# Third attention on Trainium2: scores of two heads as three fp32r products of key and query halves, keys rewritten in place, keys and values alternating

## Chip, core and metric

The kernel runs on one core of a Trainium2 chip. The metric is device time in microseconds (us) of one launch. The engines are PE (TensorE, matrix products; PEld is its weight load), ACT (ScalarE), DVE (VectorE), POOL (GpSimd) and SP (SyncE, which here issues DMA). Each runs its own instructions in order and waits for the others on semaphores.

## What is computed

Four layers, each an attention over a context of 375 rows and then a feed-forward part with experts, on x of 16 batches of 112 rows of 256. The change touches the attention of the third layer (called layer 2 in the code): 16 heads of 64, no mask.

```python
def _L2_xattn_ref(x, context, Wq, Wk, Wv, Wo, bo):
    H, DH = (16, 64)
    SCALE = DH ** (-0.5)
    b, nq, _ = x.shape
    nk = context.shape[1]
    q = (x @ Wq.T).reshape(b, nq, H, DH)
    k = (context @ Wk.T).reshape(b, nk, H, DH)
    v = (context @ Wv.T).reshape(b, nk, H, DH)
    sim = jnp.einsum('bihd,bjhd->bhij', q, k) * SCALE
    attn = jax.nn.softmax(sim, axis=-1)
    out = jnp.einsum('bhij,bjhd->bihd', attn, v).reshape(b, nq, H * DH)
    return out @ Wo.T + bo

x = x + _L2_xattn_ref(_layernorm(x, axis=-1), ctx_1024, L2_xattn_Wq, L2_xattn_Wk, L2_xattn_Wv, L2_xattn_Wo, L2_xattn_bo)
```

## The kernel before

`Att` holds what one attention layer does and in which order: its `plan` is a list of steps that every engine walks through, taking from it only what is its own. `att_tensor` turns the plan into PE's instructions, `att_vector` into DVE's, `att_scalar` into ACT's. So the place of an entry in the plan is its place on all engines at once, and an engine that waits for one entry holds up all that follow in its own list.

For the third attention (`t.halves`, since its width is 1024) the plan takes the 16 heads of a batch in eight steps of two heads, called steps 0 to 7 here. A step is, on PE:

- `scores` (L1056): for each of the two heads one fp32 matmul of 64 rows, 112 weights (queries) and 375 columns (keys). Even heads use rows 0 to 63, odd heads rows 64 to 127; the results go to banks 0 and 1. An fp32 matmul is four passes over its columns and has two records in the trace.
- `pv` (L1099): values times transposed probabilities of the two heads of two steps before.
- `turn` (L1068): transposes of the probabilities of the two heads of the step before, three pieces each.
- the `extras` of that step: projections ("gens") for the next batch and the end of the last one. Their results go to two banks in turn, 6 and 7, so that a projection waits until the one two before it has been carried off (`freed`).

The projections are: `k` (L975), one of eight key tiles, 128 x 376 in six fp32r passes (halved weights times halved context: upper times upper, upper times lower, lower times upper; fp32r is one pass over its columns); `v` (L979), one of six value tiles, 126 x 512, six such passes; `q` (L964), four of eight query tiles in fp32; `x` (L1014), transposes of two batches' normed input rows; `i` (L1001), transposes of the heads' reciprocal sums; `o` (L1005), the product with Wo; `n` (L1020), transposes of two batches' normed rows for the feed-forward part; `r` (L1027), its router. `i` is in step 1, `o` in step 3, `q` in step 0; `x` and `n` come once for two batches, `x` in step 6, `n` in step 7, `r` in the step 0 after it.

`steps` places them: `spread` deals them out over the slots of a batch by their costs, in the order queries, keys, output product, values (`post`), each not before its earliest slot.

Around the scores: DVE takes the minimum of a head's negated scores (L1285), ACT the exponential from the bank (L1327, with the row sum), PE transposes it in the next step, DVE copies that out (L1294), and `pv` uses it the step after. The scores of a head wait until the exponentials of the head two before have left its bank. After a batch's last head DVE takes the reciprocals of the sums (L1250) and spreads them over 1024 columns (L1258), which `i` transposes.

A key tile is carried off by ACT (L1373, a copy), queries by DVE (L1183, times the scale), both into buffers of two batches (`kTv`, `qmv`); values by ACT (L1379). DVE also splits the context of each batch into halves (`halve_context`, L721 and L723, in step 0), adds up the former layer's results (L763), and normalises rows (L785 for this attention, L1240 for the feed-forward part, `xn`).

Before the steps of batch 0 come its own projections: eight `k`, then six `v`, `x` and `q`. The weights of the values are halved by DVE at that point (`("wh", 1)`, `halve_values_weights`); PE's first value tile waits for it.

## Time and profile before

| | |
|---|---|
| runs | 2403.71 us median of 3 (2401.43 to 2405.17) |
| the profiled execution | 2400.26 us, of which the span of the trace is 2398.4 |
| PE busy | 2236.1 us (93%) |
| DVE busy | 1186.2 us (49%) |
| ACT busy | 1044.0 us (44%) |
| chain that ended last | PE 83%, DVE 7% |
| mean granted clock of PE | 0.97 |
| third attention | the steps with scores run from 1028 to 1722 us |

The busy shares are over the whole span. The chain that ended last is followed back from the last instruction, at each point to what released it. In a timeline each row is a start time, a duration, an engine, a line with operation and operands, and a count of instructions merged; in brackets stands how long the engine was idle before it and for what. The start of a PE row is the start of its first weight load, and PE's rows overlap a little, since a matmul's end is modelled: times between places on PE are best taken from start to start. In a table by windows, each row gives for one stretch its length, the busy time of each engine (with its count), the granted clock of PE, and DMA.

### The profile page before, as it was taken

Reading aid. Unit: us, or ns where it says so; the run is one execution under the profiler, and the core shown is the slowest. Engines: PE = TensorE matmul, PEld = TensorE weight load, DVE = VectorE, ACT = ScalarE, POOL = GpSimd, SP = SyncE. Lnnn points to the kernel's source line nnn. Section 1 sums busy time; section 2 is a strip of 40 time slices with the busy share of each in tenths; the row PEclk is TensorE's granted clock in tenths of the full one; section 3 lists DMA queues with packets and bytes.
Section 4 is the critical chain, followed back from the end, with each engine's and each line's share of the span. In section 5 each row is a group of like instructions: output and inputs, shape, how many; then the busy total and the mean of one; then the engine's idle time right before and its main releaser. Section 6 shows DMA issues by size and latency. Waiting matters only on the chain.

```text
span 2398.4 us, 44743 instructions
## 1 busy us (share of the span) xinstructions
PE 2236.1 (93%) x15310; PEld 1711.2 (71%) x15310; DVE 1186.2 (49%) x3453; ACT 1044.0 (44%) x2859; POOL 350.8 (15%) x393
## 2 busy tenths in 40 slices
PE   5999998999988899999999999999869979999998
PEld 4777877677766667777777777777647757777765
DVE  4777774222245522454554554554542256777613
ACT  3777773222223222244444444444312257778711
POOL 2000001111144255100000000000024310000020
PEclk8999998999999899999999999999979989999999
DMA  7666666222255322200000000010232177766400
GB/s 187 188 173 160 172 152 250 77 83 87 84 149 183 121 71 65 63 21 8 19 26 15 11 18 8 11 53 1 92 127 66 61 209 183 182 161 167 102 12 23
DMA packets 152698, 230.52 MB, mean 96 GB/s; under 512 B 66368, under 2 KB 127120, under 8 KB 149920
## 3 DMA queue, kind: packets, MB, share of 16 engines
q1 hardware_dynamic: 139808, 195.30, 28.5%
q0 software_dynamic: 10656, 29.37, 3.7%
q10 hardware_dynamic: 2016, 3.00, 0.5%
q8 instruction: 130, 2.13, 0.4%
q14 instruction: 88, 0.72, 0.1%
HBM read 176.36 MB, written 51.25 MB: 95 GB/s over the span
## 4 chain that ended last, share of the span: by engine, by line
PE 83%; DVE 7%; issue 3%; DMA 3%; ACT 1%; SPq 1%; POOL 1%; ACTq 0%; DVEq 0%; POOLq 0%
PE bank L1068 10%; PE bank L1859 9%; PE bank L1099 7%; PE bank L1892 6%; PE bank L979 6%; PE bank L975 6%; PE bank L1924 5%; PE bank L1005 4%; PE bank L1056 4%; PE bank L990 3%; PE bank L1051 3%; PE bank L964 3%; PE bank L1909 3%; PE bank L986 3%; PE bank L2208 2%
## 5 line engine op out<-in xcount | busy, mean ns | idle before, releaser
L1068 PE MATMUL bank<-ident,arena 112*125 112x112 f32 x2352 | 374.1, 277 | 4.6 <-ACT arena L1334 0.5
L1068 PEld LDWEIGHTS bank<-ident,arena 112*125 112x125 f32 x2352 | 336.2, 188 | 53.1 <-issue 13.1
L1327 ACT ACTIVATE arena<-arena,mx 112x375 f32<-112x375 f32 x512 | 309.5, 605 | 117.0 <-DVE mx L1273 114.6
L1273 DVE CUSTOM_DVE_ANT_0 arena<-bank,maskf 112x375 f32<-112x375 f32 x512 | 271.3, 541 | 125.9 <-PE bank L1051 124.6
L1051 PE MATMUL bank<-kS,qS 128*112 128x376 f32 x512 | 233.2, 456 | 33.6 <-DMA qS<-query_halves 24.1
L1327 ACT ACTIVATE arena<-bank,mx 112x375 f32<-112x375 f32 x272 | 156.1, 576 | 186.5 <-DVE mx L1285 155.4
L1285 DVE TENSOR_REDUCE mx<-bank 112x1 f32<-112x375 f32 x256 | 128.9, 543 | 211.8 <-PE bank L1056 211.7
L1859 PE MATMUL bank<-arena 128*128 x532 | 229.5, 554 | 2.7 <-ACT arena L1985 1.4
L1294 DVE COPY arena<-bank 125x336 f32<-125x336 f32 x448 | 214.2, 502 | 33.5 <-PE bank L1068 33.5
L1099 PEld LDWEIGHTS bank<-arena 125*32 125x32 f32 (+1 forms) x4608 | 144.5, 119 | 85.9 <-issue 68.5
L1099 PE MATMUL bank<-arena 125*32 125x112 f32 (+1 forms) x4608 | 202.6, 265 | 3.0 <-DVE arena L1294 2.9
L1334 ACT ACTIVATE arena<-bank 125x336 f32<-125x336 f32 x336 | 147.0, 438 | 47.0 <-PE bank L1068 43.4
L1892 PE MATMUL bank<-arena 128*128 (+1 forms) x672 | 167.1, 380 | 0.0
L979 PE MATMUL bank<-weight_halves,ctx_halves 128*126 128x512 f32 x576 | 150.3, 404 | 2.1 <-ACT arena L1379 2.1
L1485 POOL TENSOR_TENSOR rstd<-newton,root 112x2 f32<-112x2 f32 x32 | 22.5, 702 | 859.3 <-DVE newton L1229 859.2
L1859 PEld LDWEIGHTS bank<-arena 128*128 128x128 f32 x532 | 99.8, 191 | 65.0 <-issue 46.0
L975 PE MATMUL bank<-ctx_halves,weight_halves 128*128 128x376 f32 x768 | 143.6, 339 | 1.9 <-DVEq L715 1.9
L1924 PE MATMUL bank<-xnT,arena 128*128 128x224 f32 (+1 forms) x640 | 143.3, 369 | 0.3 <-DVEq L715 0.3
L1781 POOL DMA_INDIRECT results<-arena,scatter_id x91 | 89.9, 988 | 362.9 <-ACT arena L2007 285.0
L1051 PEld LDWEIGHTS bank<-kS,qS 128*112 128x112 f32 x512 | 91.3, 179 | 56.8 <-DMA qS<-query_halves 24.8
L975 PEld LDWEIGHTS bank<-ctx_halves,weight_halves 128*128 128x128 f32 x768 | 130.2, 188 | 2.3 <-DVEq L715 2.3
L1924 PEld LDWEIGHTS bank<-xnT,arena 128*128 128x128 f32 (+1 forms) x640 | 112.4, 181 | 24.9 <-issue 11.6
(243 smaller groups left out, 3416.4 us busy)
## 6 DMA issues: line engine op xcount, KB each, us to landing
kS<-key_halves SPq DMA_DIRECT2D x256, 188.0 KB, 3.8
key_halves<-arena SPq DMA_DIRECT2D x64, 376.0 KB, 4.1
arena<-in_ctxT SPq DMA_DIRECT2D x63, 376.0 KB, 4.5
arena<-in_f_out SPq DMA_DIRECT2D x21, 768.0 KB, 4.6
qS<-query_halves SPq DMA_DIRECT2D x256, 56.0 KB, 2.2
arena<-in_f_up SPq DMA_DIRECT2D x4, 2816.0 KB
arena<-results SPq DMA_DIRECT2D x38, 224.0 KB, 4.4
query_halves<-arena SPq DMA_DIRECT2D x32, 224.0 KB, 2.8
```

The source lines that it names most:

```text
L975: m = pe.matmul(dst[:, 0:SKE], wH[:, 0, wh, c * t.W + o * P:c * t.W + (o + 1) * P], ctxH[:, ch, c, :], **flags)
L979: m = pe.matmul(dst[0:KT + 1, 0:t.VW], ctxH[:, ch, c, o * KT:(o + 1) * KT + 1], wH[:, 1, wh, c * t.W + h * t.VW:c * t.W + (h + 1) * t.VW], ...
L1051: m = pe.matmul(bank[g % 2][0:S, 0:SKE], qS[:, b % 2, h * S:(h + 1) * S].bitcast(F32R), kS[:, b % 2, h // 2 * SKE:(h // 2 + 1) * SKE].bitc ...
L1068: m = pe.transpose(bank[2 + g % 2][0:KT, k * S:(k + 1) * S], pr[:, g % t.NR, k * KT:(k + 1) * KT], ident[0:S, 0:S])
L1099: m = pe.matmul(out, v, pTv(t, g + j)[:, k, :], **flags)
L1273: dve.tensor_tensor_reduce(sm[:, g % 2, :], bank[g % 2][0:S, 0:SK], maskf[:, :], -t.a["scale"], 3e38, ALU.add, ALU.min, mx[:, g % t.NR:g % ...
L1294: dve.tensor_copy(pTb(t, g), bank[2 + g % 2][0:KT, 0:NKT * S]).then_inc(t.pt_sbuf[1], 1)
L1327: act.activation(pr[:, g % t.NR, :], src, ACT.Exp, bias=mx[:, g % t.NR:g % t.NR + 1], scale=-1.0, accum_out=row_sum(t, b)[:, h:h + 1]).the ...
L1334: act.activation(pTb(t, g), bank[2 + g % 2][0:KT, 0:NKT * S], ACT.Copy).then_inc(t.pt_sbuf[0], 1)
L1859: ins = pe.matmul(bank[m % 2][:, 0:w * f.NU], xTb(n)[:, k, :], up[:, bass.ds(expert[n], 1), at:at + w * f.NU].rearrange("p e n -> p (e n)" ...
L1892: ins = pe.matmul(bank[4 + n % 2][:, 0:D], midT_of(f, m)[:, j * P:(j + 1) * P], w2, start=(q + j == 0), stop=(q == G - 1 and j == J - 1))
L1924: ins = pe.matmul(bank[f.hidden_bank[s]][0:w, u * 2 * S:(u + 1) * 2 * S], up[u][:, k, o:o + w], xnT[:, k, c * 2 * S:(c + 1) * 2 * S], star ...
```

## The change

Queries and keys of the third attention are held as two fp32r halves each, an upper half rounded to fp32r and the rest as lower half. The scores of a head become three fp32r matmuls that add up in its bank: upper query times upper key, upper times lower, lower times upper. They are issued for the two heads of a step in turn (bank 0 and 1), each of 64 rows, 112 weights and 376 columns. The first of the pair waits for both exponentials of the step before.

The halves: ACT writes the upper half of a key tile or of four query tiles from the bank (for queries with the scale), and DVE then writes bank minus upper half as the lower half and frees the bank. Keys have one buffer for all batches: tile o of the next batch is written over tile o of this one, and so its projection may stand only behind the scores of the pair that uses it (step o). `turns_of_keys` lays out the projections of a batch accordingly: queries, then keys and values in turn, with the output product between; each key not before slot 2o. The halving of a batch's context waits for the last key and the last value tile.

```diff
+        def turns_of_keys(w, q, k, v, out):
+            k = [(step, cost, w + 2 * step[3]) for step, cost, _ in k]
+            if not k:
+                return out
+            return (q + k[0:1] + v[0:1] + k[1:2] + v[1:2] + k[2:3] + v[2:3] + k[3:4] + out + k[4:5] + v[3:4] + k[5:6]
+                    + v[4:5] + k[6:7] + v[5:6] + k[7:8])
...
-                    spread(items + done[:cut] + post, w, H - 1)
+                    spread(items + (turns_of_keys(w, q, k, post, done[:cut]) if self.halves else done[:cut] + post), w, H - 1)
...
+        kH = within(KT_AT, "key_halves_2", [P, 2, 8, SKE], F32R)
+        qH = within(QM_AT, "query_halves_2", [P, 2, 2, 8, S], F32R)
...
-            return t.g0 + t.gen_index("v", b, NKT - 1, t.VH - 1) + 1
+            return t.g0 + max(t.gen_index("k", b, t.NO - 1), t.gen_index("v", b, NKT - 1, t.VH - 1)) + 1
...
+                    if t.halves and h % 2:
+                        continue
...
-                    elif h == 0:
-                        freed_all(pe, t, "q", b)
-                        freed_all(pe, t, "k", b)
+                    elif t.halves:
+                        if h == 0:
+                            freed_all(pe, t, "q", b)
+                        freed(pe, t, t.gen_index("k", b, h // 2))
                     if g >= 2:
-                        pe.wait_ge(t.maxed if t.masked else t.probs, t.h0 + g - 1)
+                        pe.wait_ge(t.maxed if t.masked else t.probs, t.h0 + g - 1 + t.halves)
...
                     elif t.halves:
-                        rows = slice(h % 2 * dh, (h % 2 + 1) * dh)
-                        m = pe.matmul(bank[g % 2][0:S, 0:SK], qmv(t, b)[rows, h // 2, :], kTv(t, b)[rows, h // 2, :],
-                                      start=True, stop=True)
+                        for n, (qh, kh) in enumerate(((0, 0), (0, 1), (1, 0))):
+                            for j in range(2):
+                                rows = slice(j * dh, (j + 1) * dh)
+                                m = pe.matmul(bank[j][0:S, 0:SKE], qH[rows, b % 2, qh, h // 2, :], kH[rows, kh, h // 2, :],
+                                              start=(n == 0), stop=(n == 2))
+                                if n == 2:
+                                    m.then_inc(t.scores, 1)
+                        continue
...
+                if t.halves and kind in "qk":
+                    dve.wait_ge(t.upper, t.u0 + t.upper_of[(kind, b, o, h)])
+                    if kind == "q":
+                        ins = dve.scalar_tensor_tensor(out=qH[:, b % 2, 1, o:o + t.QG, :],
+                                                       in0=src[:, 0:t.QG * S].rearrange("p (o t) -> p o t", t=S),
+                                                       scalar=qscale, in1=qH[:, b % 2, 0, o:o + t.QG, :].bitcast(F32),
+                                                       op0=ALU.mult, op1=ALU.subtract)
+                    else:
+                        ins = dve.tensor_tensor(kH[:, 1, o, :], src[:, 0:SKE], kH[:, 0, o, :].bitcast(F32), ALU.subtract)
+                    ins.then_inc(t.gen_free[n % t.GB], 1)
+                    return
...
+                if kind in "qk" and t.halves:
+                    if kind == "q":
+                        ins = act.activation(qH[:, b % 2, 0, o:o + t.QG, :],
+                                             src[:, 0:t.QG * S].rearrange("p (o t) -> p o t", t=S), ACT.Copy,
+                                             scale=-t.a["scale"])
+                    else:
+                        ins = act.activation(kH[:, 0, o, :], src[:, 0:SKE], ACT.Copy)
+                    ins.then_inc(t.upper, 1)
+                    return
...
-                elif kind == "k":
-                    ins = act.activation(kTv(t, b)[:, o, :], src[:, 0:SK], ACT.Copy)
```

What this does to the order of instructions is shown at three places. Lines of the changed kernel are some 14 to 30 higher: scores are L1075, products with values L1121, transposes of probabilities L1090, keys L989, values L993, queries L978, normed rows' transposes L1034, reciprocals' transposes L1015.

PE, step 7 of batch 2 and the scores after it (`ident,xn` is the transpose of the normed rows). Before:

```order
L1056 MATMUL bank<-arena 112x375 x2
L1099 MATMUL bank<-arena 64x112 x6
L1068 MATMUL bank<-ident,arena 125x112 x6
L979 MATMUL bank<-weight_halves,ctx_halves 126x512 x6
L1020 MATMUL bank<-ident,xn 128x112 x4
L1056 MATMUL bank<-arena 112x375 x2
```

After:

```order
L1075 MATMUL bank<-key_halves,query_halves 112x376 x6
L1121 MATMUL bank<-arena 64x112 x6
L1090 MATMUL bank<-ident,arena 125x112 x6
L989 MATMUL bank<-ctx_halves,weight_halves 128x376 x6
L1034 MATMUL bank<-ident,xn 128x112 x4
L1075 MATMUL bank<-key_halves,query_halves 112x376 x6
```

The value tile ahead of the transpose has become the last key tile, and the two matmuls of a pair have become six.

DVE from the same step 7 to the reciprocals of step 1 (`xn` is the normed rows, `lgt` the router's logits, `rinv` the reciprocals; L1294 and L1323 copy transposed probabilities). Before:

```order
L1294 COPY arena<-bank 125x336 x2
L1240 TENSOR_SCALAR xn<-x,rstd,nmr 112x256 x2
L1285 TENSOR_REDUCE mx<-bank 112x1 x2
L1294 COPY arena<-bank 125x336 x2
L763 SCALAR_TENSOR_TENSOR x<-arena,t_0,x 112x256
L721 CAST ctx_halves<-arena 128x752
L723 TENSOR_TENSOR ctx_halves<-arena,ctx_halves 128x752
L1183 TENSOR_SCALAR arena<-bank 128x448
L763 SCALAR_TENSOR_TENSOR x<-arena,t_0,x 112x256
L1207 TENSOR_TENSOR lgt<-bank,brB 112x16
L1183 TENSOR_SCALAR arena<-bank 128x448
L1250 RECIPROCAL rinv<-sums 112x16
```

After:

```order
L1209 TENSOR_TENSOR key_halves<-bank,key_halves 128x376
L1269 TENSOR_SCALAR xn<-x,rstd,nmr 112x256 x2
L1314 TENSOR_REDUCE mx<-bank 112x1 x2
L1323 COPY arena<-bank 125x336 x2
L777 SCALAR_TENSOR_TENSOR x<-arena,t_0,x 112x256
L735 CAST ctx_halves<-arena 128x752
L737 TENSOR_TENSOR ctx_halves<-arena,ctx_halves 128x752
L1204 SCALAR_TENSOR_TENSOR query_halves<-bank,query_halves 128x448
L777 SCALAR_TENSOR_TENSOR x<-arena,t_0,x 112x256
L1236 TENSOR_TENSOR lgt<-bank,brB 112x16
L1204 SCALAR_TENSOR_TENSOR query_halves<-bank,query_halves 128x448
L1279 RECIPROCAL rinv<-sums 112x16
```

The lower half of a key tile (L1209) now stands ahead of the normed rows. Those of the queries (L1204) stand where their scaling stood, the second right ahead of the reciprocals.

DVE at the start of the stage, from the first normed rows to the first scores. Before:

```order
L785 TENSOR_SCALAR on<-x,rstd,nmr 112x256 x2
L721 CAST weight_halves<-arena 128x2048
L723 TENSOR_TENSOR weight_halves<-arena,weight_halves 128x2048
L1183 TENSOR_SCALAR arena<-bank 128x448 x2
L1285 TENSOR_REDUCE mx<-bank 112x1 x2
```

After:

```order
L799 TENSOR_SCALAR on<-x,rstd,nmr 112x256 x2
L1209 TENSOR_TENSOR key_halves<-bank,key_halves 128x376 x8
L735 CAST weight_halves<-arena 128x2048
L737 TENSOR_TENSOR weight_halves<-arena,weight_halves 128x2048
L1204 SCALAR_TENSOR_TENSOR query_halves<-bank,query_halves 128x448 x2
L1314 TENSOR_REDUCE mx<-bank 112x1 x2
```

Eight lower halves of keys now stand ahead of the halving of the values' weights.

## Rows read from the trace of the kernel before

**Rows 1.** Windows over the third attention: length, engines' busy us (count), clock, DMA.
```profile
1028.00:1722.00 694.00, 686.16 (x4978) 528.79 (x4977) 351.27 (x788) 298.60 (x762) 23.86 (x28) 1.00 0.07 23
```
**Rows 2.** PE timeline, batch 4, steps 0 and 1: start, us, engine, line, count, idle before.
```profile
1201.76 0.89 PE L1056 MATMUL bank<-arena 64*112 64x375 f32 x4
...
1204.05 3.74 PE L964 MATMUL bank<-xnT,arena 128*128 128x112 f32 x32
1207.72 0.89 PE L1056 MATMUL bank<-arena 64*112 64x375 f32 x4
1208.54 0.80 PE L1099 MATMUL bank<-arena 125*64 125x112 f32 x12
1209.48 0.96 PE L1001 MATMUL bank<-ident,on 112*128 112x112 f32 x8 [0.15 <-DVE on L1258]
```
**Rows 3.** PE timeline at the start of the stage.
```profile
1005.26 8.47 PE L975 MATMUL bank<-ctx_halves,weight_halves 128*128 128x376 f32 x48 [1.86 <-DVEq L715]
1013.58 8.53 PE L979 MATMUL bank<-weight_halves,ctx_halves 128*126 128x512 f32 x36
```
**Rows 4.** PE timeline of batch 15 and the end of the stage.
```profile
1675.04 3.61 PE L1005 MATMUL bank<-arena,oT 128*112 128x256 f32 x16
...
1718.58 1.44 PE L1056 MATMUL bank<-arena 64*112 64x375 f32 x4
1719.94 0.80 PE L1099 MATMUL bank<-arena 125*64 125x112 f32 x12
...
1731.07 5.30 PE L1005 MATMUL bank<-arena,oT 128*112 128x256 f32 x16 [1.53 <-DVE oT L1175]
```
**Rows 5.** ACT timeline, second exponential of the pair at 1201.76, its sum.
```profile
1204.46 0.19 ACT L1327 ACTIVATION_READ_ACCUMULATOR arena<-bank,mx 112x1 f32 x1
```
**Rows 6.** PEld timeline, the weight loads of one pair.
```profile
1219.61 0.27 PEld L1056 LDWEIGHTS bank<-arena 64*112 64x112 f32 x4 [0.24 <-issue]
```
**Rows 7.** Groups by line and form: count, busy us, mean ns, idle before.
```profile
L1373 ACT ACTIVATE arena<-bank 128x375 f32<-128x375 f32 x128 | 62.0, 484 | 69.5 <-PE bank L975 69.4
L1384 ACT ACTIVATE xnT<-bank 128x448 f32<-128x448 f32 x64 | 34.0, 536 | 47.4 <-PE bank L1020 35.1 <-PE bank L1014 12.2
L1164 DVE TENSOR_TENSOR arena<-bank,arena 128x375 fp32r<-128x375 f32 x32 | 17.2, 538 | 1.1 <-ACT arena L1358 1.1
...
L763 DVE SCALAR_TENSOR_TENSOR x<-arena,t,x 112x256 f32<-112x256 f32 x20 | 9.1, 475 | 0.0
```
**Rows 8.** DVE timeline in step 1, second queries and the reciprocals' copy.
```profile
1207.83 0.62 DVE L1183 TENSOR_SCALAR arena<-bank 128x448 f32<-128x448 f32 x1 [1.01 <-PE bank L964]
...
1208.64 0.69 DVE L1258 COPY on<-rinv 112x1024 f32<-112x1024 f32 x1
```
**Rows 9.** ACT timeline, the copy of a key tile.
```profile
1219.72 0.48 ACT L1373 ACTIVATE arena<-bank 128x375 f32<-128x375 f32 x1 [0.54 <-PE bank L975]
```
**Rows 10.** DVE timeline in a step 7 with normed rows.
```profile
1244.69 0.73 DVE L1240 TENSOR_SCALAR xn<-x,rstd,nmr 112x256 f32<-112x256 f32 x2
```
**Rows 11.** PE timeline, batches 4 and 5: normed rows, router, rows' transposes.
```profile
1245.56 0.57 PE L1020 MATMUL bank<-ident,xn 112*128 112x112 f32 x4
...
1251.56 2.04 PE L964 MATMUL bank<-xnT,arena 128*128 128x112 f32 x16 [0.56 <-DVE arena L1183]
...
1286.00 0.55 PE L1014 MATMUL bank<-ident,arena 112*128 112x112 f32 x4
1286.85 1.66 PE L979 MATMUL bank<-weight_halves,ctx_halves 128*126 128x512 f32 x6 [0.30 <-ACT arena L1379]
```
**Rows 12.** DVE timeline at the start of the stage, halving of the values' weights.
```profile
1005.30 1.23 DVE L721 CAST weight_halves<-arena 128x2048 fp32r<-128x2048 f32 x1
1006.56 3.27 DVE L723 TENSOR_TENSOR weight_halves<-arena,weight_halves 128x2048 fp32r<-128x2048 f32 x1
```
**Rows 13.** Windows, two short stretches: the clock is third from the end.
```profile
1732.00:1734.00 2.00, 2.00 (x6) 1.49 (x5) 0.00 (x0) 0.00 (x0) 0.00 (x0) 0.50 0.00 0
1004.00:1005.00 1.00, 0.00 (x0) 0.00 (x0) 0.93 (x4) 0.00 (x0) 0.12 (x1) 1.00 0.00 0
```

More of the change, by code:

```diff
@@ L144, in __init__ @@
         self.index = {s[1:5]: s[5] for s in self.gens}
+        self.upper_of = {s[1:5]: n + 1 for n, s in enumerate(s for s in self.gens if s[1] in "qk")}
         self.in_steps = {s[1:]: n + 1 for n, s in enumerate(
@@ L149, in __init__ @@
         if self.halves:
-            self.halved = sems["halved"]
+            self.halved, self.upper = sems["halved"], sems["upper"]
+            self.u0 = 3 * B
         if self.stack:
             self.spilled, self.upper = sems["spilled"], sems["upper"]
-            self.u0 = 3 * B if L else 0
+            self.u0 = 3 * B + 10 * B if L else 0
             self.s0 = 16 * B if L else 0
@@ L285, in steps @@
                     q, k, post = self.proj(b + 1)
-                    items += ([(("ctx", b + 1), 0, 0)] if self.halves else []) + q + k
+                    if self.halves:
+                        items = [(("ctx", b + 1), 0, 0)]
+                    else:
+                        items += q + k
                 else:
-                    post = []
+                    q, k, post = [], [], []
                 if b:
@@ L291, in steps @@
                     cut = done.index((("stats", b - 1), 0, w + pv_lag)) + 1
-                    spread(items + done[:cut] + post, w, H - 1)
+                    spread(items + (turns_of_keys(w, q, k, post, done[:cut]) if self.halves else done[:cut] + post), w, H - 1)
                     follow(b - 1, done[cut:])
                 else:
-                    spread(items + post, w, H - 1)
+                    spread(items + (turns_of_keys(w, q, k, post, []) if self.halves else post), w, H - 1)
             done = self.late(B - 1, G + pv_lag)
@@ L1178, in gen @@
                     return
-                if kind in "knx" or (kind == "v" and not t.a["bv"]) or (kind == "q" and (H == 1 or t.stack)):
+                if t.halves and kind in "qk":
[9 more added lines that the diff above has]
+                    return
+                if kind in "qknx" or (kind == "v" and not t.a["bv"]):
                     return
                 dve.wait_ge(t.gen_ready, t.g0 + n + 1)
-                if kind == "q":
-                    ins = dve.tensor_scalar(qmv(t, b)[:, o:o + t.QG, :],
-                                            src[:, 0:t.QG * S].rearrange("p (o t) -> p o t", t=S),
-                                            qscale, None, ALU.mult)
-                elif kind == "v" and t.stack:
+                if kind == "v" and t.stack:
                     if b == 0 and o == 0:
@@ L1361, in gen @@
             def gen(kind, b, o, h, n):
-                if kind in "or" or (kind == "q" and H > 1 and not t.stack) or (kind == "v" and t.a["bv"]):
+                if kind in "or" or (kind == "v" and t.a["bv"]):
                     return
@@ L1368, in gen @@
                     return
+                if kind in "qk" and t.halves:
[3 more added lines that the diff above has]
+                                             scale=-t.a["scale"])
+                    else:
+                        ins = act.activation(kH[:, 0, o, :], src[:, 0:SKE], ACT.Copy)
+                    ins.then_inc(t.upper, 1)
+                    return
                 if kind == "q":
```

## The prediction

> **What bounds the kernel now.** I read the page's busy shares and its chain first: both are PE's for the most part. The change touches one stage, the third attention, so next came the windows over it: of 694 us PE is busy 686, DVE 351, ACT 299, at a granted clock of 1.00 [rows 1]. PE is the bound there: whatever shortens or delays its queue moves the end, while DVE and ACT have room on average. Then the PE timeline of one batch, which is where a wait on them would hurt. The reader should see in it that a batch is eight steps, each a pair of scores (L1056), products with values (L1099), two heads' transposes (L1068) and one to three projections, back to back, and that hardly a row carries idle time in brackets.
>
> **Scores, the gain.** A pair takes 0.82 us from its start to that of L1099 (1207.72 to 1208.54) [rows 2]. Two heads of four fp32 passes of 375 columns at 2.4 GHz are 1.25 us one after the other and 0.625 us side by side, so the two row halves do run side by side, and 0.195 us is entry and exit (the first weights, and the last columns leaving). After, each half does three single passes. One pass of this type over 376 columns has a row of its own: 48 of L975 in 8.32 us (1005.26 to 1013.58), 0.173 each [rows 3]. Is the 0.195 paid by the pair or by each of its two rounds of two passes? Where the heads of a pair ran one behind the other, four such rounds, the pair took 1.36 us (1718.58 to 1719.94) [rows 4], 0.11 above its 1.25: by the pair. So 0.195 + 3 x 0.173 = 0.71, by pure streaming (3 x 0.157) 0.665; were it by the round, 0.81. I take 0.70, near the first two: a gain of 0.12 a pair (0.11 to 0.155). It counts in the 120 pairs of batches 0 to 14: **-14.4 us** (-13 to -19). In batch 15 there are no projections, and a step is set by the exponentials: the second one ends 2.9 us after the start of its scores (from 1201.76 to 1204.46 + 0.19) [rows 2, 5], while scores, products and transposes take 2.2. Those eight I put at zero.
>
> The weights are now loaded six times a pair instead of four. The row shows the four loads done in 0.27 us [rows 6], so six would be under 0.45, hidden under the passes. The Trainium skill (TensorE: Matmul & The Clock Gate, LDWEIGHTS) gives the time of a load as its columns over 1.2 GHz, for 112 columns 93 ns. By that page's figure, six loads in line and the last pass behind them would make the pair 0.8 us, an estimate, and the gain nearly nothing; the row speaks for loads side by side.
>
> **Halving on ACT, then on DVE.** Keys were copied by ACT, queries scaled by DVE. Now ACT writes the upper half, and DVE, waiting for it, the lower. ACT: a key tile as before 0.484, and 32 new query copies of 0.536. DVE: 128 new subtractions of 0.538 [rows 7], queries 0.62 as before [rows 8]. That is 69 us more on DVE and 17 on ACT within 694, far below PE: nothing by load. What counts is how long a projection's bank (two, 6 and 7) is held, and what stands behind the halving on DVE. ACT starts 0.11 after PE has left a projection (1219.72, where PE's next work starts at 1219.61) [rows 6, 9]. DVE to PE takes 0.15 (1208.64 + 0.69 = 1209.33, to 1209.48) [rows 2, 8], for a bank some 0.10. ACT to DVE is not shown; I take 0.05, between 0 and 0.15. A key bank is free after 0.11 + 0.48 + 0.05 + 0.54 + 0.10 = **1.28 us**, against 0.69. Five places of PE's queue stand behind such a hand-over.
>
> 1. Step 1, 14 batches. PE's transposes of the reciprocals (L1001) wait for DVE's copy of them (L1258), which stands behind the second queries on DVE. The wait was 0.15 [rows 2]. DVE now starts on those queries 0.70 instead of 0.11 after they are ready, and PE arrives 0.12 sooner: 0.59 + 0.12 = 0.71, x14 = **+9.9**.
> 2. Step 7, 7 times. PE's transposes of the normed rows (L1020) wait for DVE's L1240. That ran at 1244.69 [rows 10], under a value projection, and PE went straight on at 1245.56 [rows 11]. In the new order the lower half of the last key tile stands ahead of it on DVE, and on PE nothing stands between that tile and the transposes. PE waits 0.11 + 0.48 + 0.05 + 0.54 + 0.73 + 0.15, less 0.06 of overlap, = 2.0, x7 = **+14.0**.
> 3. Step 6, 7 times. A transpose of rows (L1014, 0.55 less overlap) lies between two projections that share a bank: PE waited 0.30 [rows 11], now 1.28 - 0.50 = 0.78. 0.48 x 7 = **+3.4**.
> 4. Step 1 again: the third projection reuses the first's bank. The value tile between them takes 1.40, more than 1.28, but in 6 batches a DVE step of 0.47 (L763) [rows 7] is ahead and leaves about 0.33: x6 = **+2.0**. In the 6 batches with the router in step 0 the second queries wait on DVE already (0.56) [rows 11], so the pair's 0.12 isn't gained there: **+0.7**.
> 5. The start of the stage. Eight key tiles in a row on two banks: 1.28 against the 1.03 of the tile between, three times 0.25 = 0.75. Then the values need halved weights. DVE made them under the keys (1005.30 to 1009.83, 4.53 us) [rows 12]; the new order has them behind all eight lower halves: 0.11 + 0.48 + 0.05 + 0.54 + 4.53 + 0.10 = 5.8 of idle PE. First queries to scores: 0.59 more. Idle PE costs clock as well: 1.86 us of it before 1005.26 left the clock at 1.00 [rows 3, 13], but after the short gaps before 1731 it stood at 0.50, and L1005 took 5.30 for 3.61 [rows 4, 13]. I take that 1.7 once. **+8.8**.
>
> In the other steps no bank and no exponential is late: the shortest step, with one key tile, is 0.70 + 0.73 + 0.68 + 1.03 = 3.1, against 2.8 for both exponentials. The new wait for both at once is thus covered, by 0.3; without a projection it would cost as much as in batch 15. Rewriting keys in place adds no wait: a tile's projection stands behind its scores on PE. DMA is as before; the results of the former stage are asked for some 8 us later and are used as much later.
>
> **Sum.** 9.9 + 14.0 + 3.4 + 2.0 + 0.7 + 8.8 = 38.8, less 14.4: **+24.4 us**. The profiled execution took 2400.3 (span 2398.4); it would be 2424.7. The median of the runs is 3.4 higher, 2403.7, so I say **2428**.
>
> **Rivals.**
> - *Loads in line.* If the six loads of a pair follow one another at the 0.115 that a piece of the query projection takes (32 in 3.67 us, of which 0.093 each is streaming) [rows 2], the pair is 6 x 0.115 + 0.157 + 0.1 = 0.95, and 0.80 if half of that hides: 2440 to 2458. The skill's page above is for it, the four loads in 0.27 us against it. 8%.
> - *Halves not side by side* for this type: 0.195 + 6 x 0.173 = 1.23, +0.41 x 120 = +49 in place of -14.4: 2492. For it: no row has this type on half the rows. Against it: fp32 does it. 5%.
> - *The clock falls at the 7 waits of 2.0 us*: 1.7 each, +12: 2440. Against it: the 1.86 us at a clock of 1.00. 8%.
> - *The other side: entry and exit vanish.* If the first load and the drain hide under the neighbours (projections of the same type ahead, L1099 behind), a pair is 0.47 and the gain 0.35 x 120 = 42; 38.8 - 42 = -3: 2400.5. It ends under the time of before from 0.50 a pair on. For it: between projections nothing of the kind is paid. Against it: the 0.195 of the pairs in the trace. 7%; in more than half of that a small wait is less too, and it is over 0.2% faster.
> - *Waits half as dear* (a shorter subtraction or hand-over, no clock lost): 2406 to 2418. 12%.
> - That the change isn't made: the order shows six passes of the new type for each pair, so no.
>
> The forecast's own case, 2418 to 2440, has 60%. **Range** 2408 to 2450: halves, the dearest loads and the vanished entry are left out (some 18%), the clock is in. About 0.2% (4.8 us) is what a measurement of this kernel can tell from no change. Faster by more 5%, within it 9%, slower 86%.
>
> **What would show it.** Right: pairs 0.67 to 0.75 us long up to the values' products; PE idle in the stage up from 8 to about 45 us, with waits of about 2 us for DVE's normed rows, 0.9 for the reciprocals, and one of 5 to 6 us before the first value tile, for DVE's halving. Wrong: a pair at 0.80 or above (loads) or 1.2 (halves) or under 0.6 (entry); idle PE under 20 us; or a clock below 1.00 inside the stage after its first 30 us.

## The result, and the profile after

The changed kernel takes **2426.3 us** (median of four runs, 2423.7 to 2430.7), before 2404.4 (2401.4 to 2405.8): a ratio of 1.0102, interval 1.0089 to 1.0114 (the ratios here are the measurement's own, up to 0.0014 off the quotient of the medians, which is 1.0091 in this case). Forecast: 2428. Its profiled execution has a span of 2421.9 us, 23.5 more than before.

The first view is the windows from the start of the first scores of the third attention to that of the last, before and after: length, then busy time of PE, PEld, DVE, ACT, POOL, then the granted clock.

```profile
1027.83:1721.51 693.68, 685.85 (x4977) 528.70 (x4977) 350.78 (x787) 298.11 (x761) 23.86 (x28) 1.00 0.07 23
```
After:
```profile
1038.08:1748.80 710.72, 672.77 (x5230) 550.72 (x5231) 410.36 (x908) 310.25 (x793) 23.81 (x28) 1.00 0.07 23
```
PE is busy 13.1 us less and idle 30.1 us more (7.8 before, 37.95 after). The change does what it says, and its waits cost about twice what it saves: at full clock PE would be busy 16.9 us less, and 3.8 of these went to a slower clock (e8 below). The 23.5 us lie as follows: +1.1 before the stage, +9.1 from the first key products to the first scores, +17.0 from there to the last scores, -3.8 behind them.

The PE timeline of batches 4 and 5, after, answers to [rows 2] and [rows 11] (start, us, line, names, count, idle before and its releaser):

```profile
1209.02 1.66 PE L993 MATMUL bank<-weight_halves,ctx_halves 128*126 128x512 f32 x6 [0.77 <-DVE key_halves L1209]
...
1219.76 0.77 PE L1075 MATMUL bank<-key_halves,query_halves 64*112 64x376 f32 x6
1220.46 0.80 PE L1121 MATMUL bank<-arena 125*64 125x112 f32 x12
1222.10 0.96 PE L1015 MATMUL bank<-ident,on 112*128 112x112 f32 x8 [0.85 <-DVE on L1287]
...
1259.33 0.57 PE L1034 MATMUL bank<-ident,xn 112*128 112x112 f32 x4 [1.89 <-DVE xn L1269]
...
1265.24 2.04 PE L978 MATMUL bank<-xnT,arena 128*128 128x112 f32 x16 [0.59 <-DVE query_halves L1204]
```
A pair of scores takes 0.70 us up to the products with values (1219.76 to 1220.46), for 0.82. In exchange there is a wait at four of the places that the forecast named. Behind the last of a pair of batches' key tiles DVE first halves the tile, then writes the normed rows; DVE timeline, after, answering to [rows 10]:

```profile
1257.99 0.55 DVE L1209 TENSOR_TENSOR key_halves<-bank,key_halves 128x376 fp32r<-128x376 f32 x1 [0.90 <-ACT key_halves L1404]
1258.46 0.72 DVE L1269 TENSOR_SCALAR xn<-x,rstd,nmr 112x256 f32<-112x256 f32 x2
```
The view of PE's waits over the stage (1035 to 1746; total, times, longest):

```profile
PE bank L1034 <- DVE xn L1269: 13.2, 7, 1.9
PE bank L1015 <- DVE on L1287: 11.9, 14, 0.9
PE bank L993 <- DVE key_halves L1209: 5.4, 7, 0.8
PE bank L978 <- DVE query_halves L1204: 3.6, 6, 0.6
```
The six weight loads of a pair, on the row of PE's load queue that answers to [rows 6], take 0.44 us and lie under the products:

```profile
1219.76 0.44 PEld L1075 LDWEIGHTS bank<-key_halves,query_halves 64*112 64x112 f32 x6
```
The start of the stage, PE timeline, for [rows 3]:

```profile
1006.37 2.31 PE L989 MATMUL bank<-ctx_halves,weight_halves 128*128 128x376 f32 x12 [1.87 <-DVEq L729]
1008.95 7.24 PE L989 MATMUL bank<-ctx_halves,weight_halves 128*128 128x376 f32 x36 [0.27 <-DVE key_halves L1209]
1020.90 10.88 PE L993 MATMUL bank<-weight_halves,ctx_halves 128*126 128x512 f32 x36 [4.71 <-DVE weight_halves L737]
```
and its DVE timeline, for [rows 12]:

```profile
1017.21 1.22 DVE L735 CAST weight_halves<-arena 128x2048 fp32r<-128x2048 f32 x1
1018.46 2.29 DVE L737 TENSOR_TENSOR weight_halves<-arena,weight_halves 128x2048 fp32r<-128x2048 f32 x1
```
The long wait before the first value tile is there, and the 36 products behind it take 10.88 us for 8.53: their first third runs at clock 0.50.

One thing is there that the forecast named as a sign of being wrong, a clock below 1.00 inside the stage. Behind the third of the seven waits for normed rows the same matmuls get longer (PE timeline, after):

```profile
1351.91 0.57 PE L1034 MATMUL bank<-ident,xn 112*128 112x112 f32 x4 [1.89 <-DVE xn L1269]
1352.41 0.77 PE L1075 MATMUL bank<-key_halves,query_halves 64*112 64x376 f32 x6
1353.11 0.98 PE L1121 MATMUL bank<-arena 125*64 125x112 f32 x12
1354.02 1.60 PE L1090 MATMUL bank<-ident,arena 112*125 112x112 f32 x6
```
L1090 takes 1.60 for 0.91, and the window over it shows the clock, third from the end, at half (1.2 GHz):

```profile
1354.00:1356.00 2.00, 2.00 (x11) 1.98 (x10) 1.06 (x3) 1.13 (x4) 0.00 (x0) 0.50 0.04 15
```
It happens twice in this kernel, behind the third and the seventh of those waits.

### The profile page after: what moved, and what is told of

Same layout as the page of the kernel before. It is cut to its first block, busy times and chain, and to the rows that moved or that the text cites. A ratio compares the mean times of both kernels' runs of the same rounds, so it can differ in the third digit from the quotient of the medians.

```text
span 2421.9 us, 45521 instructions
## 1 busy us (share of the span) xinstructions
PE 2222.9 (92%) x15566; PEld 1731.2 (71%) x15566; DVE 1249.7 (52%) x3581; ACT 1055.9 (44%) x2891; POOL 349.5 (14%) x393
## 4 chain that ended last, share of the span: by engine, by line
PE 82%; DVE 8%; issue 3%; DMA 3%; ACT 2%; SPq 1%; POOL 1%; ACTq 0%; DVEq 0%; POOLq 0%
PE bank L1090 10%; PE bank L1895 9%; PE bank L1121 7%; PE bank L1928 6%; PE bank L993 6%; PE bank L989 5%; PE bank L1960 5%; PE bank L1019 4%; PE bank L978 3%; PE bank L1004 3%; PE bank L1068 3%; PE bank L1075 3%; PE bank L1945 3%; PE bank L1000 3%; PE bank L2244 2%
## 5 line engine op out<-in xcount | busy, mean ns | idle before, releaser
L1090 PE MATMUL bank<-ident,arena 112*125 112x112 f32 x2352 | 374.4, 277 | 4.9 <-ACT arena L1363 0.5
L1090 PEld LDWEIGHTS bank<-ident,arena 112*125 112x125 f32 x2352 | 336.6, 189 | 53.1 <-issue 13.4
L1323 DVE COPY arena<-bank 125x336 f32<-125x336 f32 x448 | 214.4, 502 | 19.6 <-PE bank L1090 19.5
L1121 PE MATMUL bank<-arena 125*32 125x112 f32 (+1 forms) x4608 | 203.3, 266 | 3.0 <-DVE arena L1323 2.9
L1121 PEld LDWEIGHTS bank<-arena 125*32 125x32 f32 (+1 forms) x4608 | 144.8, 119 | 49.7 <-issue 32.8
L993 PE MATMUL bank<-weight_halves,ctx_halves 128*126 128x512 f32 x576 | 155.1, 406 | 10.2 <-DVE key_halves L1209 5.4
L989 PE MATMUL bank<-ctx_halves,weight_halves 128*128 128x376 f32 x768 | 158.1, 342 | 2.6 <-DVEq L729 1.9
L1209 DVE TENSOR_TENSOR key_halves<-bank,key_halves 128x376 fp32r<-128x376 f32 x128 | 70.3, 549 | 161.2 <-ACT key_halves L1404 160.9
L989 PEld LDWEIGHTS bank<-ctx_halves,weight_halves 128*128 128x128 f32 x768 | 129.6, 188 | 12.1 <-DVE key_halves L1209 5.9
```

The costliest lines, as they stand in the source:

```text
L989: m = pe.matmul(dst[:, 0:SKE], wH[:, 0, wh, c * t.W + o * P:c * t.W + (o + 1) * P], ctxH[:, ch, c, :], **flags)
L993: m = pe.matmul(dst[0:KT + 1, 0:t.VW], ctxH[:, ch, c, o * KT:(o + 1) * KT + 1], wH[:, 1, wh, c * t.W + h * t.VW:c * t.W + (h + 1) * t.VW], ...
L1090: m = pe.transpose(bank[2 + g % 2][0:KT, k * S:(k + 1) * S], pr[:, g % t.NR, k * KT:(k + 1) * KT], ident[0:S, 0:S])
L1121: m = pe.matmul(out, v, pTv(t, g + j)[:, k, :], **flags)
L1323: dve.tensor_copy(pTb(t, g), bank[2 + g % 2][0:KT, 0:NKT * S]).then_inc(t.pt_sbuf[1], 1)
```

## Experiments

All kernels are edits of the changed one, save b1. "Idle" and "busy" are PE's between the first scores and the last. "Falls" counts the waits for normed rows behind which a window shows a clock under 0.97, of those in the stage; "behind" is the time from the last scores to the end of the span. All columns from the fourth on are of one profiled execution each, which in e5 and e8 was the slowest of eight and of ten (2409.7 and 2406.9 us), in after the fastest of four. Ratios are to before, measured beside each (2404.4 and 2404.3 for e1 to e7, 2403.0 for e8, e9 and b1).

| kernel | median us | ratio (interval) | first to last scores | idle | busy | falls | behind |
|---|---|---|---|---|---|---|---|
| before | 2404.4 | | 693.7 | 7.8 | 685.9 | | 676.9 |
| after | 2426.3 | 1.0102 (1.0089-1.0114) | 710.7 | 37.9 | 672.8 | 2 of 7 | 673.1 |
| e1 | 2425.3 | 1.0101 (1.0063-1.0140) | 712.2 | 37.9 | 674.2 | 3 of 7 | 673.5 |
| e1b | 2427.6 | 1.0100 (1.0080-1.0119) | 712.3 | 38.0 | 674.3 | 3 of 7 | 680.5 |
| e2 | 2412.8 | 1.0035 (1.0024-1.0047) | 697.1 | 27.5 | 669.7 | 0 of 7 | 673.0 |
| e3 | 2429.2 | 1.0099 (1.0082-1.0116) | 709.4 | 25.2 | 684.1 | 6 of 7 | 681.1 |
| e4 | 2392.1 | 0.9956 (0.9939-0.9973) | 677.4 | 10.2 | 667.2 | 0 of 7 | 679.9 |
| e5 | 2401.5 | 0.9983 (0.9967-1.0000) | 684.2 | 42.4 | 641.8 | 7 of 7 | 681.3 |
| e6 | 2438.3 | 1.0155 (1.0118-1.0193) | 716.5 | 37.1 | 679.4 | 3 of 7 | 680.4 |
| e7 | 2451.6 | 1.0211 (1.0173-1.0248) | 735.0 | 53.1 | 681.9 | 5 of 7 | 673.2 |
| e8 | 2403.0 | 1.0002 (0.9993-1.0012) | 684.6 | 15.7 | 669.0 | 0 of 7 | 677.4 |
| e9 | 2395.5 | 0.9964 (0.9950-0.9978) | 677.2 | 10.2 | 667.0 | 0 of 7 | 677.7 |
| b1 | 2425.0 | 1.0094 (1.0078-1.0111) | 714.7 | 19.4 | 695.3 | 6 of 6 | 677.7 |

**e5: the price of a product.**

```diff
-                        for n, (qh, kh) in enumerate(((0, 0), (0, 1), (1, 0))):
+                        for n, (qh, kh) in enumerate(((0, 0),)):
...
```


> The changed kernel with one of the three products of a head's scores, upper by upper, so two passes for a pair instead of six. The two others are left out. My theory: entry and exit (0.195 us) are paid by the pair, so it takes 0.195 + 0.17 = 0.37 us up to the values' products, against 0.70; 0.33 x 108 pairs (those ahead of a wait for DVE give nothing) = 36 us less than the change, some 2391. Rival: the cost is by the round (0.70 / 3), so the pair takes 0.23 and the time falls by 50.

PE timeline of e5:

```profile
1208.44 0.42 PE L1075 MATMUL bank<-key_halves,query_halves 64*112 64x376 f32 x2
1208.79 0.80 PE L1121 MATMUL bank<-arena 125*64 125x112 f32 x12
```
A pair with one product takes 0.35 us, with three 0.70: 0.175 a round and 0.18 of entry and exit, paid once. That is the forecast's model of a pair. But of the 42 us that 120 pairs give, only 31 are seen in PE's busy time (672.8 to 641.8): in the profiled execution the clock fell behind all seven waits. The median is 24.8 us under after's, where 36 were expected. PE's idle time grew too, since it now comes 0.35 us earlier to the reciprocals (their wait is 1.19 for 0.85).

**e6: are the halves side by side?**

```diff
-                        for n, (qh, kh) in enumerate(((0, 0), (0, 1), (1, 0))):
-                            for j in range(2):
+                        for j in range(2):
+                            for n, (qh, kh) in enumerate(((0, 0), (0, 1), (1, 0))):
```


> The changed kernel with the six products of a pair in another order: three of the first head, then three of the second. Theory: PE starts matmuls in order, so the second head's first starts only beside the first head's third: 0.31 + 0.47 + 0.195 = 0.98 us a pair, +0.28 x 108 = 30 us more than the change, some 2456. Rival: in the kernel before the pair was also written head after head, and took 0.82, as short as side by side: then 0.70 here too and no difference.

PE timeline of e6:

```profile
1206.21 0.77 PE L1075 MATMUL bank<-key_halves,query_halves 64*112 64x376 f32 x6
1206.91 0.80 PE L1121 MATMUL bank<-arena 125*64 125x112 f32 x12
```
The pair stays at 0.70 us, while six products in line would be 6 x 0.17 = 1.0. So the two row halves work side by side even where all of one head's products stand ahead of the other's. PE's idle time is after's (37.1 for 37.9). So its 12 us are not in the pairs. The profiled execution, 14.7 us longer than after's, has 6.6 us more busy time with the same matmuls and three falls of the clock, and 7.3 more behind the last scores (below). Whether this order makes the clock fall more often isn't shown.

**e2: the normed rows ahead of the last key tile.** In step 7 the transposes of the normed rows go to the front of the step's extras, so that DVE writes them before it halves the key.

```diff
-                extras[at].append(step)
+                if self.halves and step[0] == "ln" and step[2] == LN_STEPS:
+                    extras[at].insert(0, step)
+                else:
+                    extras[at].append(step)
```


> The changed kernel with one DVE step moved: in the 7 steps with a transpose of normed rows, DVE normalises the rows before the lower half of the last key tile, not after. My theory: the 7 waits of 1.9 us (13.2 us) go and nothing takes their place, since DVE is idle there while PE makes the key tile: 13 us less than the change, some 2413; with the one fall of the clock that follows such a wait in batch 15 up to 15. Rival: the key's lower half, now later, delays the minimum of the next scores and by it PE: less than 6 us gained.

PE timeline of e2:

```profile
1257.66 0.57 PE L1037 MATMUL bank<-ident,xn 112*128 112x112 f32 x4 [0.45 <-DVE xn L1272]
```
The wait is 0.45 for 1.89 (0.38 to 0.45 in all seven), PE's idle time falls by 10.5 us (7 x 1.5), and no fall of the clock is left in the stage after its start: another 3.1 of busy time. 13.5 us in the median, as expected.

**e3: the reciprocals ahead of the second queries.**

```diff
-                if last:
+                if last and g >= G:
                     plan.append(("norm", (g - 2 * lag) // H))
...
-                plan += extras[g] + extras[g + 1]
+                both = extras[g] + extras[g + 1]
+                if g and g % H == 0 and g + 2 < G + 2 * lag and g < G:
+                    at = max([n for n, s in enumerate(both) if s[:2] == ("gen", "q")] or [0])
+                    both.insert(at, ("norm", g // H - 1))
+                plan += both
```


> The changed kernel with the reciprocals and their copy (DVE) moved from behind the second queries of step 0 to ahead of them, where DVE waits for PE. My theory: the 14 waits of 0.85 us for DVE's copy (11.9 us) go: 10 to 12 us less than the change, some 2415. Rival: the second queries, then later on DVE, hold their bank, and the transposes of the reciprocals wait for that instead: under 4 us gained.

A miss: 3 us slower, not 10 to 12 faster. Yet the step did what it should. Windows, first to last scores:

```profile
1037.22:1746.57 709.35, 684.13 (x5230) 560.56 (x5231) 410.98 (x908) 310.34 (x793) 23.85 (x28) 0.98 0.07 23
```
Idle time fell by 12.7 us, all fourteen waits are gone; the same matmuls are busy 11.4 us longer. The PE timeline shows where, behind a wait of the same 1.89 us:

```profile
1256.40 0.57 PE L1038 MATMUL bank<-ident,xn 112*128 112x112 f32 x4 [1.89 <-DVE xn L1273]
1256.91 1.10 PE L1079 MATMUL bank<-key_halves,query_halves 64*112 64x376 f32 x6
1257.94 1.39 PE L1125 MATMUL bank<-arena 125*64 125x112 f32 x12
```
L1125 takes 1.39 for 0.80, and the window behind it has the clock at half:

```profile
1258.00:1260.00 2.00, 2.00 (x17) 1.72 (x16) 1.00 (x2) 0.66 (x2) 0.00 (x0) 0.50 0.26 86
```
So it goes behind six of the seven waits. From one wait for normed rows to the next, two batches, e3 needs 90.84 us where no fall is between (1535.04 to 1625.88) and 92.38 with one (1256.40 to 1348.78); after needs 92.6 without. The step gained 1.8 us per two batches, and a fall gave back 1.5, in two of the six more: there the clock stayed low for some 7 and 14 us.

**e8: e2 and e3 together**, which takes away what makes PE wait for 1.89 us.

> The changed kernel with the normed rows' transposes ahead of the last key tile (as in e2) and the reciprocals ahead of the second queries (as in e3), nothing else. Theory (the clock): in e3 the fourteen waits of 0.85 us were gone, yet the six waits of 1.89 us for the normed rows that were left were each followed by a stretch at clock 0.50, which gave 11 us back; with those waits cut to 0.39 us the clock has no reason to fall inside the stage, and e3's gain of 12.4 us shows in full on top of e2: 2412.75 - 12.4 = about 2400 us (2395 to 2407; up to 7 us more if the clock falls a few us earlier at the stage's end, as it did in e3), clock 1.00 in all of the stage after its first 30 us. Rival (e3's move itself costs what it gains, whatever the clock): 2412 to 2416 us.

```profile
1043.09:1727.71 684.62, 668.97 (x5231) 548.20 (x5231) 410.08 (x908) 310.26 (x793) 23.85 (x28) 1.00 0.07 24
```
That is e8's window from first to last scores: 12.5 us less than e2's 697.1, idle 11.8 less, no fall. The reciprocals are worth here what they were not worth in e3. The median is 3 us over the point expected and 9 under the rival's 2412; behind the last scores e8 needs 677.4, e2 673.0. With e3's same matmuls at 684.1 the falls cost e3 684.1 - 669.0 = 15 us, and after 3.8.

**b1: the wait alone, in the kernel before**, made by a reduction on DVE whose result nobody uses.

```diff
+                    if t.halves and pair < 6:
+                        dve.tensor_reduce(idle[:, pair:pair + 1], wH[0:S, 0, 0, 0:1984].bitcast(F32), AX_X, ALU.max)
                     for b in (2 * pair, 2 * pair + 1):
                         ins = dve.tensor_scalar(xnr(t, b), xb(b), rstd[:, b:b + 1], nmr[:, b:b + 1], ALU.mult, ALU.add)
```


> The kernel before, with one dead reduction over 1984 columns put into DVE's queue ahead of the normed rows of six of its pairs of batches, so that PE waits about 2 us at six places of the third attention as in the changed kernel, and nothing else is changed: no half of a key, no fp32r scores. PE idle from first to last scores goes from 7.8 to about 20 us. If only the waiting counts: 2404.4 + 12 to 14 = 2417 to 2419 us with clock 1.00 in the stage. If a wait of this size also lets the clock fall now and then (in the changed kernel after 2 of 7, in e3 after 6 of 7, 1.6 to 3.1 us each): some of the six are followed by matmuls at clock 0.50, 2420 to 2434 us.

PE timeline of b1, to be held against [rows 11]:

```profile
1251.60 0.57 PE L1021 MATMUL bank<-ident,xn 112*128 112x112 f32 x4 [2.13 <-DVE xn L1243]
1252.11 0.89 PE L1057 MATMUL bank<-arena 64*112 64x375 f32 x4
1252.92 1.10 PE L1100 MATMUL bank<-arena 125*64 125x112 f32 x12
1253.96 1.60 PE L1069 MATMUL bank<-ident,arena 112*125 112x112 f32 x6
```
Six waits of 2.13 us, and the clock fell behind each: windows, around that one and over the stage:

```profile
1254.00:1256.00 2.00, 2.00 (x12) 2.00 (x10) 0.94 (x3) 0.93 (x4) 0.00 (x0) 0.50 0.00 1
...
1028.13:1742.78 714.65, 695.28 (x4976) 535.44 (x4977) 364.26 (x793) 297.84 (x761) 23.84 (x28) 0.99 0.07 23
```
Idle time rises by 11.5, busy time by 9.4 (1.6 a fall), the kernel by 22. So neither fp32r scores nor halved keys are needed for it: a wait of this size in a PE queue that is otherwise full was enough, and cost 3.5 us, not 2.1 (21.0 over the stage, by six).

**e7: the subtraction twice**, the lower half of each key tile written two times.

```diff
...
+                        dve.tensor_tensor(kH[:, 1, o, :], src[:, 0:SKE], kH[:, 0, o, :].bitcast(F32), ALU.subtract)\
+                            .then_inc(twice, 1)
+                        dve.wait_ge(twice, b * t.NO + o + 1)
                         ins = dve.tensor_tensor(kH[:, 1, o, :], src[:, 0:SKE], kH[:, 0, o, :].bitcast(F32), ALU.subtract)
```


> The changed kernel with the lower half of each key tile computed twice on DVE, one after the other: 0.58 us more of DVE for each of 128 tiles (74 us in all), and each key bank held so much longer. My theory: the change loses time by the hand-over from ACT to DVE at certain places, so this costs 0.58 x 7 (normed rows) + 0.58 x 7 (input rows) + about 0.45 x 14 (third projection of step 1) + 2.3 at the start of the stage = 17 us more than the change, some 2443. Rival: the losses have nothing to do with DVE's part (the clock, the order of keys and values on PE): under 4 us more. Rival by load: 74 us more.

PE timeline of e7:

```profile
1220.27 1.67 PE L994 MATMUL bank<-weight_halves,ctx_halves 128*126 128x512 f32 x6 [1.35 <-DVE key_halves L1213]
...
1271.74 0.57 PE L1035 MATMUL bank<-ident,xn 112*128 112x112 f32 x4 [2.47 <-DVE xn L1273]
1272.25 1.09 PE L1076 MATMUL bank<-key_halves,query_halves 64*112 64x376 f32 x6
```
0.58 us more on DVE moves both waits by 0.58 (0.77 to 1.35, 1.89 to 2.47): DVE's subtraction is in line with PE at these places. The bank that two key tiles share is now late too (wait 6.6 us in all, 14 times). Idle time rises by 15.1 (7 x 0.58 twice, and these 6.6), busy time by 9.2, with five falls; the start of the stage takes 2.8 more. The median rises by 25.3 us where 17 were expected: the clock and the second late bank were not in that sum.

**e1 and e1b: the values' weights earlier**, ahead of all keys, or in four pieces between the key tiles.

```diff
-                ahead = [("wh", 0), ("ctx", 0)] + k + [("wh", 1)] + v + first + last + [turn] + q
+                ahead = [("wh", 0), ("ctx", 0), ("wh", 1)] + k + v + first + last + [turn] + q
```
and for e1b, with a quarter of the columns halved in each step:

```diff
+                ahead = [("wh", 0), ("ctx", 0)]
+                for n, step in enumerate(k):
+                    ahead += [step] + ([("wh", 1 + n)] if n < 4 else [])
+                ahead += v + first + last + [turn] + q
...
```


> The changed kernel with the whole halving of the values' weights on DVE ahead of the lower halves of the first eight key tiles, where it stood before the change. My theory: the wait moves from the first value tile to the third key tile, since DVE comes to the first lower half only 4.5 us after the first key tile starts, and both banks are held till then: an idle stretch of 2.5 to 4 us there, none ahead of the values, and 2 to 5 us less than the change. Rival: the halving hides under the keys as it did before the change: 8 us or more less.

> The changed kernel with the halving of the values' weights cut into four pieces, dealt out on DVE behind the first four key tiles instead of behind all eight. My theory: PE's idle stretch ahead of the first value tile (4.7 us for DVE's halving) and the slow clock that follows it (the 36 passes took 10.7 us instead of 8.4) belong to this order alone. DVE has 8 x 0.55 + 4.5 = 8.9 us of work against 8.3 us of keys on PE, so the first value tile starts some 9 to 10 us after the first key tile instead of 14.5, and no idle stretch is over 2 us: 6 to 8 us less than the 2426.3 of the change, some 2419. Rival: the stage is bound by what DVE and ACT do for the keys, so that the keys only come later by as much: no more than 2 us less.

PE timeline of e1b, start of the stage:

```profile
1016.87 2.31 PE L993 MATMUL bank<-ctx_halves,weight_halves 128*128 128x376 f32 x12 [0.22 <-DVE key_halves L1213]
1019.32 8.64 PE L997 MATMUL bank<-weight_halves,ctx_halves 128*126 128x512 f32 x36
```
The wait of 4.71 is gone and the values run at full clock (8.64): from the first key products to the first scores 26.1 us for 31.7, 5.65 less, where 6 to 8 were expected. The median does not show it (2427.6 against some 2419 expected: a miss). In the profiled execution 1.8 is lost ahead of the stage, 1.6 in the stage with a third fall, and 7.4 behind the last scores. There the rows read, in e1b

```profile
1755.46 6.71 PE L1023 MATMUL bank<-arena,oT 128*112 128x256 f32 x16 [1.53 <-DVE oT L1201]
```
and in after

```profile
1757.70 3.68 PE L1019 MATMUL bank<-arena,oT 128*112 128x256 f32 x16 [1.53 <-DVE oT L1197]
```
It is the same work behind the same wait; batch 15 ends with short waits in both, and the clock falls some 8 us behind the last scores in the one, some 18 in the other. Before it took 5.30 [rows 4]. By the start of the feed-forward part's products of `slot_ids` and `one_hots`, some 35 us on, this makes 4.0 of the 7.4; the other 3.4 come up later, and their cause wasn't looked for. e1 gains 4.3 at the start (27.4 for 31.7) and 1.0 in the median of two runs; two to five were expected. So the gain is seen at the start of the stage and not shown in the total.

e1 shows another thing at its start:

```profile
1009.43 3.81 PE L989 MATMUL bank<-ctx_halves,weight_halves 128*128 128x376 f32 x12 [1.86 <-DVEq L729]
1010.00:1012.00 2.00, 2.00 (x8) 2.00 (x7) 1.97 (x2) 0.23 (x1) 1.83 (x1) 0.50 0.07 6
```
(a row of the PE timeline and one by windows). These twelve products take 3.81 us for 2.31 in after, at half clock. They stand behind the very wait of 1.86 us that the forecast took as its evidence that such a wait leaves the clock alone.

**e4 and e9: all of it.** e4 is e8 with e1b's pieces and with the transposes of the normed input rows (step 6) moved ahead of the two projections that share a bank, between which they stood; e9 is e4 without the pieces.

```diff
-                extras[at + 4].append(turn)
+                if self.halves:
+                    at = (at + 4) // 2 * 2
+                    extras[at] = [turn] + extras[at]
+                else:
+                    extras[at + 4].append(turn)
```


> The changed kernel with the three edits above and a fourth: the transpose of input rows in step 6 stands ahead of the key tile instead of between the key and the value tile that share a bank (7 waits of 0.77 us, 5.4 us). My theory: the waits are independent, so the gains add up: 7 + 13.2 + 11.9 + 5.4 = 37.5 us less than the change, some 2389, under the kernel before by 15 us (ratio 0.994). Rival: PE is held by something else as soon as these waits are gone (the exponentials of both heads, a bank): 2400 or more, no better than before.

> e8 with the transposes of the attention output ahead of the key product (so that x is no longer between two projections that share a bank), that is, the version with all four moves but with the value weights halved in one piece. Theory: the version with all four has 677.4 us from first to last scores and 26.1 us at the stage's start; the pieces change only the start, so 677.4 here, 31.7 at the start: 2392.1 + 5.6 = about 2398 us (2391 to 2403; the lower end if the clock falls late at the stage's end, 673 us after the last scores instead of 680). Rival (the pieces help inside the stage too, through the clock or the banks): over 680 us from first to last scores and over 2403 us.

```profile
1040.80:1718.00 677.20, 666.96 (x5230) 547.94 (x5231) 410.06 (x908) 310.83 (x793) 23.85 (x28) 1.00 0.07 24
```
e9's window, like e4's 677.4, is 16 us shorter than before's, with 10.2 us idle. Both beat both kernels: before by 0.36% (e9) and 0.44% (e4). The scores were worth the change; their gain lay behind the queue order. The moves weren't tried on the kernel before, but there PE was idle for only 7.8 us of the stage, so they can't be worth the 16.5 there. The two ratios differ by 0.0008, 2 us and less than either interval, so what the pieces gain at the start (26.1 us for e9's 32.8, of which about 1 is a half clock under e9's first key products) is seen in the trace alone.

## Why the prediction was right, and where it was not

- **The pair, -14.4.** Right: 0.70 us. With the clock at 1.00 the stage's busy time falls by 16.9 (e8), somewhat more. Entry and exit are paid once (e5) and the halves run side by side in either order (e6). The rival of loads in line is out: the six loads take 0.44 us. The Trainium skill (TensorE: Matmul & The Clock Gate, LDWEIGHTS) gives a load the time of its columns over 1.2 GHz, 93 ns here; six in line are 0.56 by that, an estimate, so by the row's 0.44 they overlap in part.
- **Reciprocals, +9.9.** Right: 0.85 each, 11.9 in all, of which 0.15 each was there before. e3 took away 12.7.
- **Normed rows, +14.0.** Right in place and mechanism, a little large: 1.89, not 2.0, 13.2 in all. e7 and e2 show what it hangs on.
- **Between two projections, +3.4.** Right: 0.77 for 0.78.
- **Third projection, +2.0.** Over-sized. In the timeline of the odd batches only some 0.18 us lies ahead of it, in the even ones nothing (1.3 at most in all). The 0.7 for the router's steps came to 0.6, but not as forecast: in five of the six the queries' wait grew by 0.03 (0.59 for 0.56) and not by 0.12, and in the last by 0.42 (0.59 for 0.17).
- **The start, +8.8.** 9.1 was measured, from errors that cancel: DVE's subtraction took 2.29 us, not the 3.27 of [rows 12], so the wait was 4.7 and not 5.8; the eight key tiles took some 1.3 more than before, not 0.75, three waits of 0.4 to 0.5 each; the clock cost 2.4 there, not 1.7.
- **The clock.** This step failed. The rival "the clock falls at the 7 waits" had 8%, on the strength of one wait of 1.86 us behind which the clock stood at 1.00 [rows 3, 13]. One such wait proves nothing: behind that same wait the clock fell in two of the thirteen kernels, e1 and e9. Of 55 waits of 1.9 to 2.5 us for normed rows in eight kernels 35 had a fall behind them; of 28 waits of 0.5 or less, none. In the changed kernel it was two of seven, 3.8 us, where the rival said 12. With that the forecast's own sign of being wrong, a clock below 1.00 inside the stage after its first 30 us, came true, though the total held. That the total fits owes something to luck: from batch 0 to 14 the kernel lost 15.7 us, as the sum has it, but 1.6 of these is the clock, which hides that two waits were taken too long. PE's idle time in the stage is 37.9 us, not the "about 45" given as a sign; the forecast's own terms for the stage, 30.0 on top of 7.8, make 37.8, and only with the start does one get near 45.
- **Behind the last scores**, -3.8, was in no term. Up to some 35 us behind them it is 2.6, where the clock held until the output projection was done (3.68 for 5.30); the other 1.2 lie later and were not traced. Nor was the +1.1 ahead of the stage in a term. That these two and the errors inside the stage nearly cancel is luck.

## What to carry to other kernels

A faster instruction on the engine that bounds is worth its gain only if what hands work to that engine isn't longer: count, for each bank, the time until it is free, and look what stands behind the new step in the other engine's queue. When such a wait appears, move the step that PE waits for ahead of the new work before giving up the change: three such moves turned +1.0% into -0.4%. And take the waits together: cutting the reciprocals' waits alone (e3) showed nothing, while those for the normed rows kept pulling the clock down.

## What the hardware showed that was not expected

- A wait of about 2 us in a full PE queue can halve TensorE's clock behind it (1.2 for 2.4 GHz) for some 3 to 14 us: 1.6 us of matmul time a fall in b1, more in two of e3's. The wait itself does not decide: the same 1.89 us had a fall behind it 2 times of 7 in after, 6 of 7 in e3, 7 of 7 in e5, each counted in one execution. What does decide was not found. The Trainium skill (TensorE: Matmul & The Clock Gate, What's actually happening) says that the gate's reckoning runs on its own time, not from the kernel's start; no run here tests that.
- The part behind the last scores, the same instructions in all kernels, took 673 to 681 us, in part by where the clock fell at the stage's end (4.0 of the 7.4 between after and e1b). And the part ahead of the stage varied by 6 us between executions of the same instructions (first key products at 1005.3 to 1011.3 us). A change of 5 us at one place can't be read from the total of one execution.
- DVE's subtraction over 2048 columns took 3.27 us before and 2.29 after. Before, POOL had additions under way beside it (2.38 us), after it had none. e1, which puts the halving back under the first keys, has both again: 3.25 for the subtraction, 2.35 for POOL's additions, which take 1.29 where DVE is idle beside them. So the two engines seem to slow each other here; no run takes POOL's additions away alone.
